# Three weight slots asked for ahead of three raw slots, and the hooks of four feed-forward blocks placed anew, in a four-layer gated kernel

## The reference, cut to what matters

```python
# attention 0, 2 and 3: 16 heads of 16 columns; attention 1 ("memory") has no heads
# feed-forward 0, 1 and 3, routed (E experts of H units, K of them kept, and one shared expert of HS units)
probs    = softmax(x @ gate)                       # over the experts
combine  = the K largest of probs, elsewhere 0     # (tokens, E)
h        = silu(x @ w_gate) * (x @ w_up)           # all experts, all tokens
out      = sum over experts of combine * (h @ w_down) + shared
# feed-forward 2: relu((x @ sign(up)) * up_scale) @ sign(down)
```

## Time and profile before

| From the page | Value |
| --- | --- |
| PE busy | 1009.6 us, 88% of the span |
| DVE, ACT, POOL busy | 734.1, 573.9, 401.7 us |
| mean granted TensorE clock | 0.950 of full speed |
| chain that ended last | PE 56%, DVE 17%, DMA 9%, ACT 6%, POOL 5%, issue 5% |
| of it, DMA ff_w<-weights_out | 6% |
| DVE's idle time before L1970, ended by ff_w landing | 116.5 us in 98 instructions |
| HBM traffic | 119 GB/s over the span |

### The profile page before, as it was taken

One profiled execution on the slowest core, in us unless ns is written; L12 is line 12 of the kernel. 1 busy time (PEld: TensorE's weight loads), 2 busy tenths in 40 slices (PEclk: granted clock), 3 DMA queues, 4 the chain that ended last, 5 costly groups with the idle time before them and its releaser, 6 DMA issues.

```text
span 1149.8 us, 18125 instructions
## 1 busy us (share of the span) xinstructions
PE 1009.6 (88%) x6456; PEld 766.3 (67%) x6456; DVE 734.1 (64%) x1639; ACT 573.9 (50%) x1129; POOL 401.7 (35%) x519
## 2 busy tenths in 40 slices
PE   4799868999877997789999866799999979999998
PEld 3566537878766876665664655566655568888887
DVE  6477757557767555688887755876676254545554
ACT  3688754445334543136667432265566535544443
POOL 5524413344204434523223024324210133444443
PEclk9899989899999998779999988899999989999999
DMA  6946624474320467754521345834521153555553
GB/s 180 244 94 149 137 62 148 128 195 134 115 99 7 135 160 178 135 87 122 131 48 40 106 111 97 149 92 76 129 44 32 17 159 115 153 158 162 159 156 108
DMA packets 82067, 136.54 MB, mean 119 GB/s; under 512 B 11565, under 2 KB 40518, under 8 KB 79546
## 3 DMA queue, kind: packets, MB, share of 16 engines
q1 hardware_dynamic: 71034, 101.93, 30.0%
q0 software_dynamic: 10944, 33.45, 17.1%
HBM read 113.41 MB, written 22.97 MB: 119 GB/s over the span
## 4 chain that ended last, share of the span: by engine, by line
PE 56%; DVE 17%; DMA 9%; ACT 6%; POOL 5%; issue 5%; SPq 1%; DVEq 0%; ACTq 0%; POOLq 0%
PE psum L615 34%; PE psum L908 7%; DMA ff_w<-weights_out 6%; PE psum L875 6%; PE psum L884 5%; ACT probs L1057 2%; DVE nmx L1373 1%; DVE nmx L1370 1%; DVE psum L1975 1%; POOL keys L1120 1%; PE psum L834 1%; DVE ff_s L1970 1%; DVE nmx L1371 1%; DMA weights_out<-combine 1%; DVE probs L1464 1%
## 5 line engine op out<-in xcount | busy, mean ns | idle before, releaser
L615 PE MATMUL psum<-ff_xh,ff_wh 128*128 128x512 f32 x424 | 176.3, 416 | 25.8 <-POOL ff_wl L1931 16.9
L1059 ACT ACTIVATE probs<-psum 128x512 f32<-128x512 f32 x256 | 144.1, 597 | 76.6 <-PE psum L875 73.0
L875 PE MATMUL psum<-queries,keys 128*128 128x512 f32 x384 | 154.9, 434 | 11.4 <-ACT probs L1057 5.9
L615 PE MATMUL psum<-ff_xh,ff_wl 128*128 128x512 f32 x392 | 156.4, 399 | 0.0
L1970 DVE TENSOR_TENSOR ff_s<-psum,ff_w 128x512 f32<-128x512 f32 x98 | 67.6, 689 | 126.3 <-DMA ff_w<-weights_out 116.5
L1931 POOL TENSOR_TENSOR ff_wl<-ff_raw,ff_wh 128x512 fp32r<-128x512 f32 x92 | 119.0, 1295 | 70.8 <-ACT ff_wh L1883 70.1
L1872 ACT ACTIVATE ff_hh<-psum 128x512 fp32r<-128x512 f32 x114 | 67.9, 596 | 143.0 <-DVE psum L1975 142.2
L615 PE MATMUL psum<-ff_wh,ff_hh 128*128 128x256 f32 x456 | 131.4, 292 | 4.8 <-DVE ff_hl L1985 4.6
L884 PE MATMUL psum<-keys,queries 128*128 128x512 f32 x256 | 117.1, 474 | 17.4 <-DVE nmx L1371 8.8
L615 PE MATMUL psum<-ff_wh,ff_hl 128*128 128x256 f32 x456 | 130.6, 290 | 0.0
L1936 POOL TENSOR_TENSOR ff_wl<-ff_raw,ff_wh 128x256 fp32r<-128x256 f32 x92 | 68.7, 746 | 172.1 <-ACT ff_wh L1890 172.1
(11 more groups left out here) (263 smaller groups left out, 2173.0 us busy)
## 6 DMA issues: line engine op xcount, KB each, us to landing
ff_w<-weights_out SPq DMA_DIRECT2D x94, 256.0 KB
ff_raw<-in_ff SPq DMA_DIRECT2D x92, 256.0 KB, 4.1
ff_raw<-in_ff SPq DMA_DIRECT2D x106, 128.0 KB, 2.2
keys_out<-keys_turned SPq DMA_DIRECT2D x24, 512.0 KB, 3.7
keys<-keys_out POOLq DMA_DIRECT2D x48, 256.0 KB, 5.0
queries_out<-queries_turned SPq DMA_DIRECT2D x24, 256.0 KB, 3.5
keys<-keys_out POOLq DMA_DIRECT2D x48, 128.0 KB, 5.4
queries<-queries_out POOLq DMA_DIRECT2D x32, 192.0 KB, 4.0
```

The costliest lines, as they stand in the source:

```text
L615: last = eng.matmul(dst, lhs[i](k), rhs[j](k), start=start and n == 0, stop=stop and n == groups * len(pairs) - 1, skip_group_check=True)
L875: then(eng.matmul(dst, kst[buf(c)][:, pair, kt * P:(kt + 1) * P], qst[buf(c)][:, :, pair, :], start=True, stop=True, skip_group_check=True ...
L1059: ins = eng.activation(dst, src, ACT.Exp, scale=SCALE)
```

## The change

There are three raw slots and three slots of combine weights. The third one takes the place of the fourth raw slot. SP asks for the combine weights of step n+1 ahead of the raw tile n+3. Nine numbers of the hooks and of the planner change.

```diff
-RAWS = 4
+RAWS = 3
+
+WEIGHTS = 3
@@ HOOKS
-         4: [("late", "wn")], 5: [("statistics", 1), ("normal", 1)],
-         6: [("turn", 1), ("halves", 1)], 8: [("logits", 1), ("route", 1, 0), ("route", 1, 1)],
+         4: [("late", "wn")], 5: [("statistics", 1)], 6: [("normal", 1)],
+         7: [("turn", 1), ("halves", 1)], 9: [("logits", 1), ("route", 1, 0), ("route", 1, 1)],
...
-         0: [("weights", 0), ("combine", 0), ("statistics", 1)], 1: [("normal", 1)],
+         0: [("weights", 0), ("combine", 0), ("extra", 0), ("statistics", 1)], 1: [("normal", 1)],
...
-         3: [("late", "wn")], 4: [("statistics", 1)], 5: [("normal", 1), ("extra", 0)],
-         6: [("turn", 1), ("halves", 1)], 9: [("add", 0)]},
+         3: [("late", "wn")], 4: [("statistics", 1)], 5: [("normal", 1)],
+         6: [("turn", 1), ("halves", 1)], 9: [("add", 0), ("extra", 0)]},
...
-         3: [("statistics", 1), ("normal", 1)], 4: [("turn", 1)], 5: [("halves", 1)],
-         6: [("logits", 1)], 7: [("route", 1, 0)], 8: [("route", 1, 1)], 9: [("route", 1, 2)],
-         10: [("weights", 1)], 12: [("combine", 1)], 26: [("add", 0)]}]
+         3: [("statistics", 1)], 4: [("normal", 1)], 5: [("turn", 1)], 6: [("halves", 1)],
+         7: [("logits", 1)], 8: [("route", 1, 0)], 9: [("route", 1, 1)], 10: [("route", 1, 2)],
+         11: [("weights", 1)], 13: [("combine", 1)], 26: [("add", 0)]}]
@@ LEADS, attention 3
-         3: {7: [("au", 0), ("kp", 0, 0), ("sq", 0, 0), ("ms", 0, 0)],
-         8: [("kk", 0, 0), ("tk", 0, 0), ("te", 0, 0)],
-         10: [("kp", 0, 1), ("sq", 0, 1), ("ln", 0), ("ms", 0, 1), ("kk", 0, 1)],
-         11: [("tk", 0, 1), ("te", 0, 1), ("kw", 0), ("lm", 0)], 12: [("xt", 0), ("xe", 0)],
-         13: [("q", 0)], 14: [("sq", 0, 2), ("ms", 0, 2), ("kk", 0, 2), ("tq", 0), ("qe", 0)]}}
-
-SENDS = {2: [("kw", 14), ("qw", 18)], 3: [("kw", 15), ("qw", 15)]}
+         3: {7: [("kp", 0, 0), ("sq", 0, 0), ("ms", 0, 0)],
+         8: [("au", 0), ("kk", 0, 0), ("tk", 0, 0), ("te", 0, 0)],
+         10: [("kp", 0, 1), ("sq", 0, 1), ("ln", 0), ("ms", 0, 1), ("kk", 0, 1), ("lm", 0)],
+         11: [("xt", 0), ("xe", 0), ("tk", 0, 1), ("te", 0, 1), ("kw", 0)],
+         12: [("q", 0), ("sq", 0, 2), ("ms", 0, 2), ("kk", 0, 2)], 13: [("tq", 0), ("qe", 0)]}}
+
+SENDS = {2: [("kw", 14), ("qw", 18)], 3: [("kw", 13), ("qw", 13)]}
@@ the routing's place in the planner's order
-FOLLOW = {0: (17.6, 4.6, 20), 2: (30.2, 9.2, 0), 3: (25.6, 9.2, 25.6)}
+FOLLOW = {0: (17.6, 4.6, 13), 2: (30.2, 9.2, 0), 3: (25.6, 9.2, 16)}
@@ DVE, weighted(n, slot)
-                eng.wait_ge(sems[f"d_fw{slot}"], (n // 2 + (ff_before(f, f"d_fw{slot}") + 1)) * 16)
+                s = n % WEIGHTS
+                eng.wait_ge(sems[f"d_fw{s}"], (n // WEIGHTS + (ff_before(f, f"d_fw{s}") + 1)) * 16)
...
@@ SP
         def load_weights(eng, n):
-            slot, h = n % 2, half_of(n)
-            w(eng, "f_sw", n - 1)
+            slot, h = n % WEIGHTS, half_of(n)
+            w(eng, "f_sw", n - WEIGHTS + 1)
...
             for n in range(first, last + 1):
+                if not sign:
+                    if n == 2:
+                        load_weights(eng, n)
+                    if n + 1 == tiles:
+                        weights_out(eng, 1)
+                    if n + 1 < N:
+                        load_weights(eng, n + 1)
                 if 2 + RAWS <= n + 3 < N:
                     load_tile(eng, n + 3)
-                if not sign:
-                    load_weights(eng, n)
-                    if n == tiles - 1:
-                        weights_out(eng, 1)
@@ POOL's program
-        eng.wait_ge(sems["c_pv"], T)
-        zero_stack(eng, qst[FIRST_BUFFER[2]])
-        ff[1][2](eng, None, heads2)
+        def queries_cleared(_):
+            eng.wait_ge(sems["c_pv"], T)
+            zero_stack(eng, qst[FIRST_BUFFER[2]])
+
+        ff[1][2](eng, None, heads2, queries_cleared)
```

More of the change, by code:

```diff
@@ L490, in flamingo @@
             "xl": [at(f"ff_xl{i}", k + 12288, [P, KC, HALF], F32R), xl_second],
-            "s": at(f"ff_s{i}", q, [P, 2, HALF]), "w": at(f"ff_w{i}", q + 4096, [P, 2, HALF]),
+            "s": at(f"ff_s{i}", q, [P, 2, HALF]), "w": [at(f"ff_w{i}{n}", q + 4096 + 2048 * n, [P, HALF]) for n in range(2)] + [ff_w2],
             "hh": at(f"ff_hh{i}", q + 8192, [P, 2, HALF], F32R),
@@ L1570, in counts @@
             return 0
-        if kind in ("d_fw0", "d_fw1"):
-            return TILES[f]
+        if kind in ("d_fw0", "d_fw1", "d_fw2"):
+            return len(range(int(kind[4]), n, WEIGHTS))
         return {"f_sd": n, "f_uf": n, "f_sw": n, "f_w1r": n, "f_w2r": n, "f_rt": 2, "f_re": 2,
@@ L1966, in weighted @@
             def weighted(n, slot):
-                eng.wait_ge(sems[f"d_fw{slot}"], (n // 2 + (ff_before(f, f"d_fw{slot}") + 1)) * 16)
+                s = n % WEIGHTS
+                eng.wait_ge(sems[f"d_fw{s}"], (n // WEIGHTS + (ff_before(f, f"d_fw{s}") + 1)) * 16)
                 w(eng, "f_sd", n + 1)
-                then(eng.tensor_tensor(ff_s[:, slot, :], psum[:, GATE_BANKS[slot], :], ff_w[:, slot, :], ALU.mult), "f_sw")
+                then(eng.tensor_tensor(ff_s[:, slot, :], psum[:, GATE_BANKS[slot], :], ff_w[s][:, :], ALU.mult), "f_sw")
             def gated(n, slot):
@@ L2074, in load_weights @@
         def load_weights(eng, n):
-            slot, h = n % 2, half_of(n)
-            w(eng, "f_sw", n - 1)
+            slot, h = n % WEIGHTS, half_of(n)
+            w(eng, "f_sw", n - WEIGHTS + 1)
             if n % tiles < ones:
-                eng.dma_start(ff_w[:, slot, :], a["one"].to_broadcast([P, HALF])).then_inc(sems[f"d_fw{slot}"], 16)
+                eng.dma_start(ff_w[slot][:, :], a["one"].to_broadcast([P, HALF])).then_inc(sems[f"d_fw{slot}"], 16)
                 return
@@ L2082, in load_weights @@
             src = wm[f][h][bass.ds(n % tiles, 1), :, :].rearrange("one g (r c) -> (one g) r c", r=1)
-            eng.dma_start(ff_w[:, slot, :], src.to_broadcast([RUNS, RUN, HALF])).then_inc(sems[f"d_fw{slot}"], 16)
+            eng.dma_start(ff_w[slot][:, :], src.to_broadcast([RUNS, RUN, HALF])).then_inc(sems[f"d_fw{slot}"], 16)
         def sp_weights(eng):
```

5 lines of the change are left out of this document (3 added, 2 removed).

## The result

Median 1125.35 us of four runs (1123.53 to 1126.91), against 1156.86 before (four runs, 1154.7 to 1158.51): a ratio of 0.9728, 95% interval 0.9706 to 0.9751. That is 31.5 us; the forecast said 34 and 1123.5. The profiled execution took 1123.53 us (span 1121.7). It lies 1.8 us under the median, that of before 5.3 under its own; the two spans differ by 28.1 us.

The account below looks back on a forecast made before the run. PE bounds the kernel (88% of the span); winnable are its idle times where stages meet and half-clock stretches after them. Terms sum to 35.9 us, less 2 gives 34: 1157.5 - 34 = 1123.5 us, range 1110 to 1137.

Parts of the forecast that it names:

- Weights a step ahead: Earlier ff_w ends PE's 6.74 us stall in feed-forward 1 (gain 8.8 us) and smaller idle times elsewhere (6.7 us).
- keys_out: First keys go out after lo_down(14), so PE stands 4.5 us at gate(16) of feed-forward 1; cost 6.4 us, bounds 2.5 and 9.
- Three raw slots elsewhere: Up pieces asked for a step later cost 0; at the change of halves +1 us for both blocks, bounds -4 and 2.
- The memset: Clearing moved from ahead of lo_up(0) into hook 0 of feed-forward 1: 1.7 us of idle time and 0.8 of clock.
- the turns: Roots and second halves in feed-forward 3 and 0: norm ready a step later, less PE waiting; 6.7 us together, bounds 1 and 9.
- Routing of attention 3: Combine sent some 8 us earlier frees raw tiles 2 and 3 of feed-forward 3; gain 6.5 us, bounds 3 and 7.
- Routing of attention 0: Routing 7 positions up: exponential waits for DVE's token update, last score 1 us later; cost 1, bounds -2 and 4.
- First keys and queries of attention 3: Weight splits and constant rows behind POOL's root, query's norm in hook 12; waits of 7.74 and 3.18 us shrink; gain 11.1 us.
- C: Rival: slower, 1170 us; three raw slots starve the splits and lengthen PE's steps; chance 0.04.
- D: Rival: the weights do nothing beyond what their waits show, hooks alone count; 20 us won, 1137 us; chance 0.15.
- B: Rival: more than forecast, 1103 us; keys_out lands in 4.3 us, no low-clock stretch follows the remaining idle times; chance 0.10.
- A: Rival: half the gain, 1142 us; each idle time is replaced by the next wait, as stages meet in transfers; chance 0.13.

Follow-up runs that it names:

- order_alone: hooks_only with one more edit: on SP the weights of step n are asked for ahead of raw tile n+3; 1124.11 us, ratio to before 0.9753.
- hooks_only: The kernel before with every part of the change but the loads (four raw slots, two weight slots, old SP order); 1138.60 us, ratio 0.9856.
- keys_early: The changed kernel with the first keys of attention 2 sent after SP's step 13, not 14; 1130.07 us, ratio to before 0.9788.
- halves_order: The changed kernel with raw tile n+3 asked for ahead of load_weights(n+1) at the change of halves; 1125.10 us, ratio to before 0.9755.
- follow3_back: The changed kernel with the routing of attention 3 back at its old place (25.6, not 16); 1133.48 us, ratio to before 0.9834.
- the three pairs: Kernels differing only in attention 0's routing place, 13 against 20; ratios to before 0.9728 and 0.9725, 0.9753 and 0.9714, 0.9755 and 0.9709.

## Why the prediction was right, and where its steps were not

The sum held (34 forecast, 31.5 measured, 28.9 when run again), and so did the mechanism of its largest parts. Routing in attention 0, the queries of attention 3 and the change of halves gave less than forecast, the routing of attention 3 more. That 34 came so near has some luck in it: the terms add up to 35.9, the two profiles differ by 28.1, 1.1 of that lie at the start, where no term stood, and the change would have been worth about 5 us more without one of its own parts.

- **Weights a step ahead, 8.8 and 6.7.** Right as a mechanism: ff_w(16) is in time, and the idle times at 190.85, 410.31, 432.15 and 461.09 of the earlier trace rows are gone or under 1 us, but for the transposes at step 18 in the second profile. "About 1 us of waiting" for ff_w(17) was the best case: DVE waited 2.18 us in one profile and 6.43 in the other, and feed-forward 1 gained 8.9 or 2.4 us where 8.4 were forecast. The step failed in treating a landing time as one number in a stretch where the DMA share is 0.96 to 1.06. The cause, an earlier request, was right; order_alone adds that the place on SP gives it alone, without the third slot.
- **keys_out, cost 6.4.** The place (gate(16)) and the releaser were right; PE stood 2.7 us, not 4.5. lo_down(14) ended 4 us earlier than in the trace of before, since the waits for weights ahead of it were gone, and POOL had keys_out 5.2 us after the send, not 5.9 (which is no mean of 4.3 and 6.4; that is 5.35). With 1.6 us of clock the cost was about 4. The Trainium skill ("DMA: Bandwidth & Descriptors", Queues, rings and completion order) led to 4.3 for a send with no weights just ahead of it. In direction the traces agree: with ff_w sent 0.64 us ahead (before and hooks_only) the first of the two sends landed after 4.9 and 4.8 us and POOL had both after 6.4; with no weights within 3.7 us ahead (twelve profiles) it landed after 3.0 to 4.1, and POOL had both after 4.9 to 6.1. The size, 1.6 us, was too large for what POOL sees, 1.2. keys_early shows that taking this wait away brought no time.
- **Three raw slots elsewhere.** Cost 0 in the steady part: right. At the change of halves the sign was wrong: not 1 us won, but from 70 to 100 us into feed-forward 0 PE's idle time is 4.9 us for 2.7 (3.5 in the second profile). The raw tile stands on SP behind load_weights(n+1), which waits until weights_out has landed; this held raw tile 16 until 245 us, and halves_order, which takes it out of that place, has 2.0 us of idle time there. And not seen at all: other loads behind the raw tiles come later too. This would have cost some 4 us in feed-forward 2, had the change not moved the root.
- **The memset, 2.5; the turns, 6.7.** The 1.74 us at the first gate of feed-forward 1 went, but 0.73 came back at once as a longer wait for gate_lo (last section), and half-clock time took more in some profiles (attention 1 got 1.7 and 0.6 us shorter in the two of the changed kernel). In feed-forward 0 the turns still wait on POOL's lo_up: 2.43 us at 205.55 for the 2.58 and 0.40 of before, where 1.4 were to be won. In feed-forward 3 they are gone.
- **Routing of attention 3, 6.5.** It was 8 in the profile of follow3_back.
- **Routing of attention 0, cost 1.** The step that failed, outside its own bounds of -2 to 4 in the first profile. The exponential did wait for DVE's token update as foreseen, but in attention 0 it costs 3.4 to 4.7 us: the last score came 120.2 us after the first instead of 114.5, so 5.7 us later, not 1. PE stood twice (2.17 and 1.92 us) and then worked at half clock from 151.0 to 157.8 and from 164.6 to 174.9 (6.8 us in all before). Up to the last score the first profile has 2.3 us more idle time and 6.8 us more at half clock than before. In hooks_only, order_alone, halves_order and follow3_back, as long up to that point, it is 3.8 to 4.2 us more idle time and 3.4 us more at half clock. So the forecast had both too low, the waits and the clock; and it left out feed-forward 0, where the three pairs have another 1.8 to 3.6 us.
- **First keys and queries of attention 3, 11.1.** The two waits came out as worked through: 2.08 us for 7.74 (forecast: under 3) and 0.99 for 3.18 (0.7). The earlier layer norm costs about what was forecast: 1.91 us at 671.20 in place of a wait of 1.27 for the key's norm at the same step. Two things were off. The first maximum still waits 5.36 us (5.63 before), where 1.2 were to be won. And a wait not seen grew: 2.47 us at 664.66 for 1.24. It ends with DVE's sums, two of which took 0.70 and 1.03 us in place of 0.48, beside the weight splits that the change moved there (last section). 6 to 8 us remain.

Of the rivals, C did not appear (PE's step unchanged). D falls: the loads alone won 9.4 us and the whole change more than D's 20. B's stretches at the low clock did go in feed-forward 3 (none left where the profile of before had 13.7 us of them). A's reason is seen at the end of feed-forward 1, where a wait taken away came back a step or two later.

Four slips in the working changed nothing in the forecast. The stretches at the low clock from 457.0 and 665.2 did not follow the waits of 6.74 and 7.74 us; they began 2.6 and 2.9 us after PE had stopped, while it still stood. Rival A's lower bounds are not the ones stated with the terms (-4 for the raw slots, 4 for attention 0), by which its sum is -1.3 and not 4. Rival B's gains add up to 50 us, which is a median of about 1107.6 and not 1103. And work at the low clock takes less than twice its time: in the trace after, matmuls on 512 columns start every 427 ns there and every 229 at the full clock, on 256 columns every 213 and 120, so the cost is 0.44 to 0.46 of PE's busy time.

## What to carry to other kernels

On a queue that works in order, ask what waits ahead of the transfer that is late: swapping two requests gave what a third buffer gave. Fewer buffers delay not only their own loads but every load behind them in that queue, so look at which other stage's inputs stand there. Before pulling a send forward, read the DMA share of the stretch that it lands in: here, at 0.96 to 1.06, the stall moved and no time was won. And a part of a change that wins as a whole can still lose: it was seen only when each part was put back alone, in more than one pair.
